# Node pipeline of a graph network kernel: three layers in row and column groups of TensorE, root and linear layer ahead of the last blend, six early pairs instead of eight

## The reference, cut to what matters

```python
h = relu(layernorm(x));  x = x + (relu(h @ Wr_in.T + b) @ Wr_out.T + b)        # first convolution, 32 -> 64 -> 32
h = relu(layernorm(x));  x = x + relu(relu(relu(h @ W1 + b1) @ W2 + b2) @ W3 + b3)   # 32 -> 128 -> 128 -> 32
h = relu(layernorm(x));  s = relu(h @ lin0.T + b)
for _ in range(6):                                                              # GRU with a constant message
    r, z = sigmoid(...s @ hr), sigmoid(...s @ hz)
    n = tanh(in + r * (s @ hn));  s = (1 - z) * n + z * s
x = x + s
```

## Time and profile before

| | us |
|---|---|
| median of 3 runs | 10505.85 |
| lowest, highest | 10487.84, 10520.05 |
| the profiled execution | 10524.02 |
| its span in the trace | 10522.1 |
| mean granted clock of PE in it | 0.821 of full speed |
| PE busy | 7195.7 |
| DVE, ACT, POOL busy | 4806.5, 2489.1, 3507.0 |

### The profile page before, as it was taken

How to read it: one execution, slowest core, us unless ns; L and a number is a source line. 1 busy time by engine, 2 the same in 40 slices (tenths; PEclk the granted TensorE clock), 3 DMA queues, 4 the chain that set the end, 5 groups by cost and what they waited for, 6 DMA issues and landing times.

```text
span 10522.1 us, 68844 instructions
## 1 busy us (share of the span) xinstructions
PE 7195.7 (68%) x20977; PEld 3018.6 (29%) x20986; DVE 4806.5 (46%) x6600; ACT 2489.1 (24%) x3922; POOL 3507.0 (33%) x3839
## 2 busy tenths in 40 slices
PE   3648777754306878978687878687575588888860
PEld 1323333322203332222222222222243344444420
DVE  4324422211315445557575757576364444444440
ACT  1324422211102221111111111111321134444430
POOL 4742044355472333334343434343512400000016
PEclk9868777777558998989898989898787788989875
DMA  2000044456665347768686868687211200000000
GB/s 67 7 5 12 22 146 150 151 77 64 82 36 119 68 80 202 216 187 231 189 231 186 231 192 233 188 232 198 35 14 18 8 14 8 12 10 10 8 11 19
DMA packets 529332, 1044.71 MB, mean 99 GB/s; under 512 B 100335, under 2 KB 273859, under 8 KB 528580
## 3 DMA queue, kind: packets, MB, share of 16 engines
q1 hardware_dynamic: 411652, 965.27, 26.3%
q0 software_dynamic: 117312, 75.04, 14.6%
HBM read 825.33 MB, written 215.22 MB: 99 GB/s over the span
## 4 chain that ended last, share of the span: by engine, by line
PE 54%; issue 14%; DVE 13%; another core or an unknown queue 7%; POOL 4%; DMA 4%; ACT 3%; SPq 0%; DVEq 0%; POOLq 0%; ACTq 0%
PE ps L920 9%; PE ps L834 5%; PE ps L1174 3%; PE ps L896 3%; PE ps L1024 3%; POOL gathered L704 3%; PE ps L1018 2%; PE ps L1019 2%; PE ps L1010 2%; PE ps L1013 2%; PE ps L908 2%; PE ps L1000 2%; DVE ring L1875 1%; DVE scan L1782 1%
## 5 line engine op out<-in xcount | busy, mean ns | idle before, releaser
L704 POOL DMA_INDIRECT gathered<-table,idx_slot x2288 | 2215.7, 968 | 1982.6 <-DVE ring L1875 1031.0
L920 PE MATMUL ps<-ring,mats 128*32 128x512 f32 x4160 | 1123.6, 667 | 438.3 <-DVE scan L1782 258.3
L1875 DVE TENSOR_TENSOR ring<-ring,ps 128x1024 f32<-128x1024 f32 x1040 | 1240.8, 1213 | 300.2 <-DMA ring<-net 202.7
L834 PE MATMUL ps<-mats,gathered 128*128 128x128 f32 x1092 | 202.1, 318 | 781.4 <-DMA gathered<-table,idx_slot 594.8
L1942 DVE SCALAR_TENSOR_TENSOR blocks<-ps,bias,ring 128x512 f32<-128x512 f32 x300 | 225.1, 751 | 1100.0 <-PE ps L1024 972.5
L834 PE MATMUL ps<-mats,w 128*128 128x128 f32 x1404 | 277.3, 344 | 513.8 <-DVE w L2298 256.8
L813 POOL COPY idx_slot<-idx_run_end 128x16 int32<-128x16 int32 x13 | 2.6, 196 | 1819.1 <-SPq L686 1802.5
L920 PEld LDWEIGHTS ps<-ring,mats 128*32 128x32 f32 x4160 | 212.4, 117 | 1241.1 <-issue 662.2
L1174 PE MATMUL ps<-w,en 128*128 128x512 f32 x832 | 463.0, 709 | 118.1 <-ACT ring L1591 60.6
L697 POOL COPY idx_slot<-idx_row 128x16 int32<-128x16 int32 x143 | 29.2, 204 | 1462.2 <-SPq L496 1191.8
L1817 DVE SCALAR_TENSOR_TENSOR w<-ps,bias,w 128x512 f32<-128x512 f32 x156 | 117.0, 750 | 744.6 <-PE ps L1345 417.6
(11 more groups left out here) (271 smaller groups left out, 13052.4 us busy)
## 6 DMA issues: line engine op xcount, KB each, us to landing
ring<-net SPq DMA_DIRECT2D x1248, 512.0 KB
net<-ring SPq DMA_DIRECT2D x208, 512.0 KB
table<-w SPq DMA_DIRECT2D x195, 256.0 KB, 2.9
gathered<-table,idx_slot POOLq DMA_INDIRECT x2496
x_sp<-x_block SPq DMA_DIRECT2D x117, 256.0 KB
x_block<-x_sp SPq DMA_DIRECT2D x117, 256.0 KB
d_block<-d_sp SPq DMA_DIRECT2D x104, 256.0 KB
d_block<-d_sp POOLq DMA_DIRECT2D x52, 256.0 KB, 3.2
```

The costliest lines, as they stand in the source:

```text
L704: pool.indirect_dma_start(dests(k), None, rows, bass.IndirectOffsetOnAxis(ap=dst[:, k:k + 1], axis=0)).then_inc(done, 16)
L834: last = nc.tensor.transpose(dst[:, k * P:k * P + P], src[:, k * P:k * P + P], mat["ident"])
L920: last = mm(message[t * D:t * D + D, :], adders[2 * m + c], ring[slot][:, c * W:c * W + W], start=(m == 0 and c == 0), stop=(m == PAIRS // ...
L1875: v.tensor_tensor(pair, pair, state, ALU.mult).then_inc(sig["pr"][S_], 1)
```

## The change

Five things are changed, all inside `nodes`, and one constant.
1. In `conv(n, t)` chain c takes quarter (t + c) mod 4. Its inner product uses only the 32 rows of that quarter, its last product writes only the 32 rows of the result that belong to the quarter. The two chains' inner products stand directly behind each other, in different row groups, and so do the last products, in different column groups. For both the code waits for both chains first.
2. The inner layer of the first convolution uses 64 rows for each of its two products, its output layer writes 64 rows with each.
3. The third norm of a pair (spread, transpose, multiplication) and its linear layer are done at the end of the period in which the norm's statistics are made, ahead of blend 5 of the pair before; until now they stood at the start of the next period. The two other spreads come after blend 5.
4. The output is transposed into `front_a` instead of `gate_b`, the gates of step 0 come directly behind it on PE, ahead of the transposes of the two other norms. ScalarE's Relu of the linear layer also waits for the final addition, because the state is still read by it. ScalarE takes the square root ahead of the tanh of step 5.
5. `EARLY` is 6.

```diff
-EARLY = 8
+EARLY = 6
...
+        lower, upper = slice(0, 2 * D), slice(2 * D, 4 * D)
...
                 def conv(n, t):
+                    quarter = [slice((t + c) % T * D, (t + c) % T * D + D) for c in range(CHAINS)]
                     for c in range(CHAINS):
                         ready(pe, "aC", c, q.n("aC", c, n))
-                        mm(front_a[c], wt[f"w1_{t}"], n_b[n % 2][c], start=True, stop=True).then_inc(sig["q1"][c], 1)
+                    for c in range(CHAINS):
+                        mm(front_a[c], wts[quarter[c], WEIGHTS.index(f"w1_{(t + c) % T}"), :], n_b[n % 2][c][quarter[c], :],
+                           start=True, stop=True).then_inc(sig["q1"][c], 1)
                     for c in range(CHAINS):
                         ready(pe, "q1r", c, q.n("q1r", c, n, t))
                         mm(front_a[c], wt["w2"], n_low[c], start=True, stop=True).then_inc(sig["q5"][c], 1)
                     for c in range(CHAINS):
                         ready(pe, "q6", c, q.n("q6", c, n, t))
-                        mm(front_b[c], wt[f"w3_{t}"], n_high[c], start=(t == 0), stop=(t == T - 1)).then_inc(sig["q7"][c], 1)
+                    for c in range(CHAINS):
+                        mm(front_b[c][quarter[c], :], wts[:, WEIGHTS.index(f"w3_{(t + c) % T}"), quarter[c]], n_high[c],
+                           start=True, stop=True).then_inc(sig["q7"][c], 1)
...
                     if done is not None:
                         for c in range(CHAINS):
                             ready(pe, "of", c, q.n("of", c, done))
-                            turn(gate_b[c], n_change[c]).then_inc(sig["ot"][c], 1)
-                    if d is not None:
-                        ready(pe, "ln_r", 0, q.n("ln_r", 0, d))
-                        for c in range(CHAINS):
-                            turn(gate_a[c], spread_in[0][:, c * W:c * W + W]).then_inc(sig["tD"][c], 1)
+                            turn(front_a[c], n_change[c]).then_inc(sig["ot"][c], 1)
+                    if d is not None:
+                        gates(d, 0)
...
-                    if d is not None:
-                        for c in range(CHAINS):
-                            ready(pe, "aD", c, q.n("aD", c, d))
-                            if done is not None:
-                                ready(pe, "oc", c, q.n("oc", c, done))
-                            mm(gate_b[c], wt["lin0"], n_c[c], start=True, stop=True).then_inc(sig["lin"][c], 1)
-                        gates(d, 0)
                     if b is not None:
                         for c in range(CHAINS):
                             ready(pe, "aB", c, q.n("aB", c, b))
-                            mm(front_a[c], wt["l0_r0"], n_a[c], start=True, stop=True)
                             if m is not None:
                                 ready(pe, "aC", c, q.n("aC", c, m))
-                            mm(front_b[c], wt["l0_r1"], n_a[c], start=True, stop=True).then_inc(sig["l0b"][c], 1)
+                            mm(front_a[c], wt["l0_r0"][lower, :], n_a[c][lower, :], start=True, stop=True)
+                            mm(front_b[c], wt["l0_r1"][upper, :], n_a[c][upper, :], start=True, stop=True).then_inc(sig["l0b"][c], 1)
...
-                            mm(front_a[c], wt["l0_or0"], n_low[c], start=True, stop=False)
-                            mm(front_a[c], wt["l0_or1"], n_high[c], start=False, stop=True).then_inc(sig["l0x"][c], 1)
+                            mm(front_a[c][lower, :], wt["l0_or0"][:, lower], n_low[c], start=True, stop=True)
+                            mm(front_a[c][upper, :], wt["l0_or1"][:, upper], n_high[c], start=True, stop=True).then_inc(sig["l0x"][c], 1)
...
                     if d is not None:
                         hidden(d, 5)
+                    if m is not None:
+                        ready(pe, "ln_r", 0, q.n("ln_r", 0, m))
+                        for c in range(CHAINS):
+                            if d is not None:
+                                ready(pe, "rh", c, q.n("rh", c, d, STEPS - 1))
+                            turn(gate_a[c], spread_in[0][:, c * W:c * W + W]).then_inc(sig["tD"][c], 1)
+                        for c in range(CHAINS):
+                            ready(pe, "aD", c, q.n("aD", c, m))
+                            if d is not None:
+                                ready(pe, "z", c, q.n("z", c, d, STEPS - 1))
+                            mm(gate_b[c], wt["lin0"], n_c[c], start=True, stop=True).then_inc(sig["lin"][c], 1)
...
                             ready(act, "lin", c, q.n("lin", c, d))
+                            if done is not None:
+                                ready(act, "of", c, q.n("of", c, done))
                             f(n_state[c], gate_b[c], ACT.Relu, bias=one_col("lin0_b")).then_inc(sig["hn"][c], 1)
...
-                    if d is not None:
-                        new(d, 5)
...
                         f(n_root[:], n_var[:], ACT.Sqrt).then_inc(s_root, 1)
+                    if d is not None:
+                        new(d, 5)
...
-                    if d is not None:
-                        apply(gate_a, "tD", n_c, "aD", d)
...
                     if d is not None:
                         reset(d, 5)
-                        blend(d, 5)
-                        for c in range(CHAINS):
-                            ready(dve, "hn", c, q.n("hn", c, d, STEPS))
-                            v.tensor_tensor(n_change[c], n_x[d % 4][c], n_state[c], ALU.add).then_inc(sig["of"][c], 1)
...
                         if m is not None:
                             spread(spread_in[0], LN3, "ln_r")
-                        if a is not None:
-                            spread(spread_in[1], LN1, "bB")
-                        if b is not None:
-                            spread(spread_in[2], LN2, "bC")
+                            apply(gate_a, "tD", n_c, "aD", m)
+                    if d is not None:
+                        blend(d, 5)
+                        for c in range(CHAINS):
+                            ready(dve, "hn", c, q.n("hn", c, d, STEPS))
+                            v.tensor_tensor(n_change[c], n_x[d % 4][c], n_state[c], ALU.add).then_inc(sig["of"][c], 1)
+                    if a is not None:
+                        spread(spread_in[1], LN1, "bB")
+                    if b is not None:
+                        spread(spread_in[2], LN2, "bC")
```

More of the change, by code:

```diff
@@ L1037, in nodes @@
                         for c in range(CHAINS):
+                            if done is not None:
+                                ready(pe, "oc", c, q.n("oc", c, done))
                             turn(front_a[c], spread_in[1][:, c * W:c * W + W]).then_inc(sig["tB"][c], 1)
@@ L1967, in nodes @@
                             stored(dve, "st_out", c, first + done)
-                            v.tensor_copy(n_out[c], gate_b[c]).then_inc(sig["oc"][c], 1)
-                    if d is not None:
-                        apply(gate_a, "tD", n_c, "aD", d)
+                            v.tensor_copy(n_out[c], front_a[c]).then_inc(sig["oc"][c], 1)
                     if b is not None:
```

## The result

| | before | changed |
|---|---|---|
| median, us (6 runs each, on one chip) | 10499.01 | 10573.45 |
| lowest, highest | 10487.66, 10520.05 | 10549.64, 10592.43 |
| ratio | | 1.0069, 95% interval 1.0049 to 1.0088 |
| the profiled execution, its span | 10524.0, 10522.1 | 10592.4, 10590.6 |

A forecast was written before the change was run, and what follows sets the result against it. PE was taken as close to full, its work nearly equal to the PE-ScalarE ladder. +0.8 us a period gave +17, early pairs -2: median 10506 + 15, forecast 10520 us; range 10450 to 10600, the forecast's own 10470 to 10570.

The forecast's parts named there:

- gain and losses nearly even: Whole kernel: the forecast's own case, gains and losses almost cancel, 10470 to 10570 us, chance 0.52.
- rival 3: Convs: one more fall to the low clock per period than counted, +3.5 us each, 10595 us; chance 0.2.
- Tiled products, +0.8: Four convs and gates 4: PE's saved work becomes waiting for ScalarE's Relus, +0.8 us a period.
- First convolution, +0.1: Its output layer, between hidden 0 and gates 1: no gain, shape changes cost +0.1 us a period.
- The turn, -1.5: Gates 5 to hidden 0: gates 0 start 3.45 us sooner, part given back behind them, -1.5 us a period.
- some 4 us: Gates 0 at the turn: time until the clock rises, at 0.85 us a record until then.
- Clock in the convs, +1.4: Convs: holes in PE's work make the clock fall more often and for longer, +1.4 us a period.
- the ladder: Each conv: PE and ScalarE alternate, products waiting for Relus; a step takes 5.67 us instead of 5.60.
- nearly all periods, 2 to 3 us each, less the 0.8 us that I put on a mean period now: Convs: how often and how much the low clock costs, net of its present cost, giving +1.4 us a period.
- Six early pairs, -2: Early and late stages: two full periods fewer early save 203 us, two more late cost 2 x 100.3, together -2 us.
- GpSimd's 32 us of gathers in each, which would then lie beside the draining periods: Early stage: gathers of the two dropped periods move beside the draining ones; 200 to 225 us saved, 203 taken.

The follow-up runs named there:

- convs alone: Kernel before the change, with only the tiled products of conv() added: 10546.20 us, ratio 1.0052.
- holes filled: Changed kernel plus an unread 352-column product ahead of the middle and of the last products of each conv: 10564.84 us, ratio 1.0086.
- old conv, new turn: Changed kernel with conv() back to full-size products, six early pairs kept: 10494.23 us, ratio 1.0009.
- gathers held: Changed kernel with one more GpSimd wait, for the output of early pair 2, ahead of the gathers that follow the setup: 10550.83 us, ratio 1.0066.
- two useless products: Changed kernel plus one unread 256-column product behind conv 1 and one behind conv 3: 10541.35 us, ratio 1.0064.

## Why the prediction was right and where it was off

The range held, but the mechanism "gain and losses nearly even" did not: the forecast was too good by 53 us, by 59 if the change is compared (+15 against +74), and 10573 lies 3 us above the forecast's own 10470 to 10570. What kept the time inside the range is its upper edge, which was put there for rival 3, the clock; two thirds of the error come from the early pairs, for which no rival had a price between -2 and +200 us. So that it held is in part luck. Turn, tiles and clock went in the direction that the sum gave them, the early pairs did not come out even. The clearest view is a period cut into stretches by the starts of PE's products (chain 0), averaged over the 11 to 13 full late periods of each profiled execution (without the first two), in us:

| stretch | before | convs alone | changed | holes filled | old conv, new turn |
|---|---|---|---|---|---|
| gates 5 to gates 0 | 29.3 | 29.6 | 26.5 | 26.3 | 25.7 |
| gates 0 to hidden 0 | 7.0 | 7.0 | 8.6 | 10.1 | 9.2 |
| hidden 0 to gates 2 | 18.1 | 18.1 | 18.2 | 18.2 | 18.2 |
| gates 2, conv 0 | 12.0 | 12.9 | 13.2 | 12.9 | 12.1 |
| conv 1 | 7.8 | 8.0 | 9.0 | 8.0 | 7.8 |
| conv 2, conv 3, gates 4 | 26.2 | 26.9 | 26.9 | 26.9 | 26.2 |
| period | 100.3 | 102.4 | 102.4 | 102.4 | 99.2 |

- *Tiled products, +0.8.* Right in mechanism, and small. Where the clock is full they cost 0.21 (conv 1) and 0.71 us (the last stretch), in conv 0 0.09 (12.89 us in convs alone, 12.80 in the cold periods before): +1.0. PE has 5.6 us less to do and all of it becomes waiting. What the Trainium skill, "TensorEngine Tiling (Array Packing)", section "Performance Considerations", says of evacuation is what happens here: the Relus behind the products are the bound.
- *First convolution, +0.1.* As forecast: hidden 0 to gates 2 is 18.22 us instead of 18.11.
- *The turn, -1.5.* From gates 5 to hidden 0 it is 36.57 to 35.10 us in the two periods shown, -1.47. Against the mean period before (36.3) it is -1.2. The extra table load, 1.28 us of ScalarE, is covered. How long gates 0 stay cold, "some 4 us" in the sum, is not one number in the runs: in the changed kernel it is their first two records of eight (1.57 us instead of 1.13), with the holes filled five. PE's wait ahead of the output's transposes is 2.81 us where the sum had 1.8.
- *Clock in the convs, +1.4.* Mis-sized. Conv 0 and 1 are 2.4 us longer, some 0.3 of it the ladder: +2.1. The step that failed is "nearly all periods, 2 to 3 us each, less the 0.8 us that I put on a mean period now": it is every period, at 2.8 us (1.8 in conv 0, 1.0 in conv 1), less 0.7. The mean granted clock in late periods is 0.90 in both kernels (twelve periods of the kernel before, fourteen of the changed one, and fourteen of the changed one with the old conv for comparison):

```profile
8742.50:9945.80 1203.30, 1030.20 (x2881) 503.52 (x2881) 557.05 (x890) 574.98 (x900) 0.00 (x0) 0.90 0.03 10
```
```profile
8576.70:10011.90 1435.20, 1126.49 (x3360) 506.14 (x3360) 653.40 (x1038) 685.07 (x1064) 0.00 (x0) 0.90 0.03 10
```
```profile
8549.20:9938.20 1389.00, 1173.42 (x3360) 543.13 (x3360) 652.77 (x1037) 686.68 (x1064) 0.00 (x0) 0.92 0.03 11
```

Next to the kernel before the low stretches did not take more time, they came to lie where PE's products are on the path: conv 0 is cold in every period, in the kernel before in 5 of 11 (12.8 us against 11.3). Next to the old conv on the new turn, at 0.92, the tiled convs do cost clock: the turn had given some back, and they took it again. Rival 3's mechanism, more falls, was nearer than the forecast, with the price of 2.1 - 1.4 = 0.7 us and not of 3.5.
- Together +2.1 us a late period where the sum had 0.8: 18 us in all. (Between the first and the last reciprocal of the late stage it is 1897.8 us, before 1666.2: 231.6 more, where 200.6 for two more periods and 16 times 0.8, together 213, were expected.)
- *Six early pairs, -2.* This is the larger error, 40 us. The step that failed: "GpSimd's 32 us of gathers in each, which would then lie beside the draining periods". They do not; they bunch in period 4 (+54 us there), and held back they cost as much in a draining one. The kernel before with six early pairs shows the same loss alone, 10527 against 10486 us. Late, two pairs cost 204.8 us, and the early stage ends 159 us sooner where -203 and 5 times 0.8 gave 199.
- Sum: 15 forecast, + 18 + 40 = 73, measured 74 in the medians. The two terms are read from the profiled executions, which differ by 68 us; the rest of the program takes 4 us less there.

Still open is what fixes a period at 102.4 us in five kernels (the changed one with six and with eight pairs, gathers held, convs alone, holes filled; the first three have the same late stage, so there are three different ones). Seen is that a gain in one stretch came back as cold products in another: -1.3 us in the convs and +1.3 at the turn for the fillers. Seen is also that in these kernels the half clock comes at the same place of every period: in the changed kernel from 46.8 to 53.7 us behind the reciprocal, conv 0 and 1, in twelve periods running. Period and clock keep step. In the kernel before, with periods of 99.9 to 100.5 us, the half clock moves within the period, and misses conv 0 in 6 of 11.

What makes the clock fall in conv 0 is open too. That the holes let it fall was the theory; it is not shown, and the holes alone do not do it. The clock also falls there with full-size products and with filled holes, only for a shorter time. And it does not always fall with the holes open: conv 0 is warm in 7 of 13 periods of the kernel with two useless products, and in the first full late period of the one with the gathers held (99.4 us). That kernel's late stage is the changed one's instruction for instruction, and there the same period takes 102.0 us with a cold conv 0. The Trainium skill, "TensorE: Matmul & The Clock Gate", section "Part 1: The HAM clock gate", says that the gate's watch runs free of the program, so that the same kernel can meet it in another phase. That would fit the same instructions being warm in one period and cold in the next, and falls that only change their place; no run here moves the phase by itself, so it is not shown.

## What to carry to other kernels

When products are made shorter and each has an evacuation behind it, look at the ladder first: here 5.6 us less of PE's work became waiting, and the order that puts a product of the GRU into each hole of the convs, and the reverse, took 7.6 us off a late period with full-size products (99.0 to 91.4, eight early pairs) and 12.5 with tiles (102.4 to 89.9). How much of this is covered waiting and how much the higher granted clock (0.94 instead of 0.92 with full-size products, 0.93 instead of 0.90 with tiles) was not separated. A transfer or gather that seems to run beside other work has a price by how closely it is bunched; before moving pairs of work between stages, count it in both. Judge a change at a granted clock near 0.9 by which work lies in the low stretches, not by the mean, and measure the parts alone: their ratios added up here within their intervals, the terms within a period did not.

## What was not expected of the hardware

- Periods lock: 102.4 us, equal to 0.1 us over a dozen periods, in five kernels with three different late stages. With conv 0 in full size 99.1, 102.3 and 102.4 us return in turn. With 0.86 us of useless products on the path a mean period was 100.5 us in the one profiled execution, at a granted clock of 0.91 instead of 0.90.
- Gathers of GpSimd beside a full pipeline cost 11 to 14 us for 32 in a period, 46 for 64 (142.3 against 96.4), 114 for some 110 (216.2 against 102.4), while VectorE's and ScalarE's busy times stay at 45 to 51 us. By GpSimd's own busy time that is 0.35 to 0.42, 0.73 and 1.07.
- Useless products in waits of 3.1 and 2.7 us raised the granted clock from 0.93 to 0.96 and took 1.5 us off a period; in the 0.74 and 0.87 us holes of the changed kernel's convs they moved the low stretch and gained nothing.
